# A fused two-layer transformer on one core: the opening of its second attention, reordered

## The reference, cut to what matters

```python
x = x + L0_attn(ln(x))   # 16 heads of 8, rope, softmax, then a relu FFN
x = x + L0_ffn(ln(x))    # router picks 2 of 16 experts: 128 -> 512 -> 128, relu
x = x + L1_attn(ln(x))   # causal attention with an added "incidence" bias
x = x + L1_ffn(ln(x))    # router picks 2 of 8 experts, exact gelu
```

```python
logits = q @ k.T * 8 ** -0.5 + (r @ (J w).T) * decay[h] ** (tq - tk) * bias_scale[h]   # bias only for tq > tk
attn   = softmax(where(tk > tq, -inf, logits))
```

## Time and profile before

| what | us |
|---|---|
| three runs | 1718.39, 1709.72, 1717.89; median 1717.89 |
| the profiled execution | 1723.04 |
| its span, first to last instruction | 1721.3 |
| TensorE busy | 1436.0 (83%), mean granted clock 0.92 |
| VectorE busy | 1237.4 (72%) |
| ScalarE busy | 934.4 (54%) |
| GpSimd busy | 694.0 (40%) |

### The profile page before, as it was taken

The page is one execution under the profiler, slowest core; times in us unless marked ns, Lnnn a source line. Parts: engine busy times, 40 slices in busy tenths (PEclk is TensorE's granted clock), DMA queues, the critical chain, the costliest instruction groups (busy, mean ns, idle before and its releaser), DMA issues. The chain is left out here.

```text
span 1721.3 us, 38302 instructions
## 1 busy us (share of the span) xinstructions
PE 1436.0 (83%) x11726; PEld 955.6 (56%) x11726; DVE 1237.4 (72%) x4218; ACT 934.4 (54%) x1914; POOL 694.0 (40%) x812
## 2 busy tenths in 40 slices
PE   3899999999999945999248989898898987838993
PEld 1224333443333335999126667676776765628993
DVE  5777888888886544555578697888989796635555
ACT  2477777777775712665235555556555553305561
POOL 3123443534422334555225344535454460234552
PEclk8799999999998977999669999999999999968997
DMA  6211111111111061222453444444344453042225
GB/s 159 73 43 61 47 55 47 51 59 51 55 48 41 14 233 51 73 72 64 138 171 122 131 143 138 132 137 143 117 136 140 136 151 115 14 135 62 71 73 165
DMA packets 122424, 166.42 MB, mean 97 GB/s; under 512 B 21490, under 2 KB 96018, under 8 KB 121586
## 3 DMA queue, kind: packets, MB, share of 16 engines
q1 hardware_dynamic: 113330, 145.69, 29.2%
q0 software_dynamic: 8896, 18.30, 3.2%
HBM read 116.04 MB, written 47.60 MB: 95 GB/s over the span
## 5 line engine op out<-in xcount | busy, mean ns | idle before, releaser
L1124 DVE TENSOR_REDUCE a_M<-a_F 128x1 f32<-128x512 f32 x512 | 325.3, 682 | 87.5 <-PE a_F L1318 85.4
L1025 ACT ACTIVATE L_W<-a_ST 128x512 f32<-128x512 f32 x512 | 276.8, 595 | 89.5 <-PE a_ST L1359 88.8
L2042 ACT ACTIVATE L_W<-c_ST 128x1024 f32<-128x1024 f32 x160 | 163.0, 1019 | 175.4 <-PE c_ST L2432 129.2
L2654 ACT ACTIVATE L_hT<-L_P,L_W1s 128x128 f32<-128x128 f32 x600 | 171.4, 367 | 143.1 <-PE L_P L2735 110.9
L2640 POOL DMA_INDIRECT L_yd<-L_ys,L_di x150 | 163.5, 1090 | 151.2 <-DVE L_ys L2686 147.4
L489 POOL DMA_INDIRECT L_xd<-L_XN,L_place_i x128 | 124.6, 973 | 144.4 <-issue 93.5
L1359 PE MATMUL a_ST<-L_W 74*128 74x512 bf16 x512 | 167.0, 390 | 14.2 <-ACT L_W L1025 7.5
L1318 PE MATMUL a_F<-L_W 72*128 72x512 bf16 x512 | 165.0, 398 | 7.9 <-DVE a_M L1124 7.1
L2726 PE MATMUL L_P<-L_xT,L_W1s 128*128 128x128 f32 x1200 | 161.1, 278 | 0.0
L2735 PE MATMUL L_P<-L_W,L_hT 128*128 x1200 | 159.2, 276 | 0.1
L2431 PE MATMUL c_ST<-ident,c_SD 128*128 128x128 f32 x512 | 147.5, 288 | 13.5 <-ACT L_W L2042 13.5
(11 more groups left out here) (430 smaller groups left out, 3090.5 us busy)
## 6 DMA issues: line engine op xcount, KB each, us to landing
c_QS<-c_q SPq DMA_DIRECT2D x32, 504.0 KB
c_QS<-c_rd SPq DMA_DIRECT2D x32, 378.0 KB
L_xg<-L_xd SPq DMA_DIRECT2D x150, 64.5 KB
L_W<-a_q SPq DMA_DIRECT2D x32, 288.0 KB
L_W<-a_k SPq DMA_DIRECT2D x96, 96.0 KB
L_W<-c_k SPq DMA_DIRECT2D x96, 96.0 KB
L_W<-in_L_w SPq DMA_DIRECT2D x8, 1024.0 KB, 12.9
c_QI<-c_r SPq DMA_DIRECT2D x32, 216.0 KB
```

What stands on the lines that cost most here:

```text
L1025: act.activation(PT[:, j, kk, :], ST[:, kk, :], ACT.Exp).then_inc(sem(exped), 1)
L1124: dve.tensor_reduce(M[:, t, h:h + 1], FB[n % BANKS][:, :], AX_X, ALU.max).then_inc(sem(maxed), 1)
L2042: act.activation(PT[:, j, :, :], ST[:, :, :], ACT.Exp).then_inc(sem(exped), 1)
L2654: act.activation(hT[:, n % 2, f, :], PS[2 + 2 * (n % 2) + f // 2][:, (f % 2) * P:(f % 2 + 1) * P], func, bias=W1s[:, n % WB, F + f:F + f + ...
```

## The change

Four things change. (1) The loads of the first two of the five batches are issued ahead of the wait for the weights; the other three stay behind it. (2) VectorE runs mix(0) and mix(1) ahead of the products of batch 0, and not between measure(1) and scale(1). (3) In the opening SyncE stores three of the five pieces of lines, waits for r and w, issues the points of quad 0, then stores the two rd pieces, and fills the c_wd stack and the c_rd stack with a wait for the rd stores between; that is the order in which `run` has it for the later batches. (4) In `run`, the points of quad 1 of the next batch are issued (after the wait for the logits of quad 3) ahead of the wait for quad 2's scores and of quad 2's stacks, and no longer ahead of quad 3's.

```diff
             sp.dma_start(rd_d[:, :, 0:P].rearrange("a p s -> p a s"), QS[0:LINES, 0:PARTS, 0:P]).then_inc(weights, 16)
+
+            def load_results(n):
+                i = B - LATER + n
+                for k in range(CH):
+                    sp.dma_start(mixing[:, n, k, :, :], results[:, k, i * T:(i + 1) * T, :]).then_inc(mix_loaded[n], 16)
+
+            for n in range(2):
+                load_results(n)
             sp.wait_ge(weights, 16 * NW)
...
-            for n in range(LATER):
-                i = B - LATER + n
-                for k in range(CH):
-                    sp.dma_start(mixing[:, n, k, :, :], results[:, k, i * T:(i + 1) * T, :]).then_inc(mix_loaded[n], 16)
+            for n in range(2, LATER):
+                load_results(n)
             store_qk(0)
             stack_qk(0, 0)
-            store_lines(0, range(5))
+            store_lines(0, range(3))
             lines_stored(0, 0)
             stack_points(0, 0)
+            store_lines(0, range(3, 5))
             lines_stored(0, 1)
+            stack_written(0, 0)
             lines_stored(0, 2)
-            stack_lines(0, 0)
+            stack_read(0, 0)
             stack_points(0, 1)
...
                     for g in range(1, NQ):
-                        if g == NQ - 1:
+                        if g == 2:
                             quad_logits(i, 3)
                             stack_points(i + 1, 1)
                         quad_scored(i, g)
...
+            for n in range(2):
+                mix(n)
             for z in range(2):
                 products(dve, 0, z)
                 sums(0, z)
...
             measure(1)
-            for n in range(2):
-                mix(n)
             scale(1)
             for n in range(2, LATER):
                 mix(n)
```

## The result

| | before | after |
|---|---|---|
| median of 21 runs each, us | 1721.30 | 1713.14 |
| lowest and highest | 1708.77, 1738.44 | 1702.66, 1729.96 |
| ratio, 95% interval | | 0.9952, 0.9929 to 0.9975 |
| profiled execution, its span | 1723.04, 1721.3 | 1720.21, 1718.1 |
| second attention, from the first weight's load to the expert layer's first weights | 677.4 | 665.0 |

A forecast was written before the change was run, and what follows sets the result against it. Opening bound by no engine, its end set by the c_rd stack's DMA; later batches keep TensorE and VectorE nearly gapless. Terms +0.1, +0.1, 0, +0.4, -0.8 sum to -0.2 us: 1717.7 us from 1717.89, range 1709.5 to 1723.0.

The forecast's parts named there:

- signs of being wrong: Forecast falls if batches from 934 us on differ by over 1 us each; other signs covered projections, c_rd stack, first logits.
- the bands given: Signs of being right in the opening: c_rd stack issued at 879.4 to 880.2, TensorE's first logits at 885.8 to 886.6.
- What bounds the opening: 833 to 886 us: no engine bounds it; the c_rd stack's DMA releases the first logits, VectorE has 3.39 us of slack.
- Four loads: Loads ahead of the weights' wait may delay the last weights' landing: +0.1 us, bounds 0 and 3.5.
- rival 1: Early loads crowd the weights in the opening and delay the projections: up to 3.5 us, 1721.2 us; chance 0.16.
- Sixteen adds in the gap: Adds in VectorE's gap before batch 0's products: products slip 0.5 us, mostly absorbed; +0.1 us, bounds 0 and 1.3.
- The adds gone from before the scale: VectorE, 874.22 to 880.34 us: it waits for GpSimd's rstd instead; value 0, bounds 0 and 0.3 us.
- rival 3: The adds before the scale were the gate: 6.1 us go, 1711.8 us; chance 0.06.
- First stacks: Opening's stores and stacks in the batches' order: c_rd stack 0.4 us later, bounds 0.6 sooner and 1.0 later.
- Points of quad 1 in each batch: Issued before quad 2's scores in each batch, they save at most the 1.2 us of waits: -0.8 us, bounds -1.2 and 0.
- Rival 4: The new median falls on the level of one earlier run, with nothing gained by the change: 1709.5 us; chance 0.14.

The follow-up runs named there:

- e2: Kernel before with parts 1 to 3 (early loads, early adds, first stacks' order), run's order as before; 1722.57 us, ratio 1.0040.
- e3: Kernel before with only the early loads and early adds (parts 1 and 2); ratio 0.9953, median of all ten runs 1718.05 us.
- e6: Changed kernel with the next batch's quad 2 points also ahead of quad 3's scores; 1708.17 us, ratio 0.9931 against the kernel before.
- e4: Kernel before with only the first stacks in the batches' order (part 3); ratio 1.0022.
- e10: Kernel before, but in run(6) quad 1's points go between the two halves of quad 2's stacks; one run, 1715.45 us beside 1721.06.
- e5: Kernel before with quad 1's points ahead of quad 2's scores in run(6) alone; 1714.33 us, ratio 0.9961.

## Why the prediction was right and wrong, by its steps

That the time lies in the range is luck. The forecast started from a median of three runs that was 3.4 us too low, and its change was -0.2 us where 8.2 were measured; the low end that caught the result was there for spread alone. Its own signs of being wrong point the same way: I had no mechanism by which a batch could differ by more than 1 us, and the last one differed by 7.4; and no wait for c_KI was to stay, where 4.5 us in 4 did. Counted as in the trace before, the c_rd stack went out at 880.4 and the first logits started at 887.4, 0.2 and 0.8 us later than the bands given.

- *What bounds the opening*: right. The c_rd stack released the first logits after as before, and VectorE had slack (4.52 us).
- *Four loads*: right in size. The first projections came 10.16 us after the first weight's load, against 10.05 before; rival 1 (crowded weights) is out: no trace has them later than 10.65.
- *Sixteen adds in the gap*: right in the changed kernel, low in the others. The adds took 4.54 us (4.5 said), ended 0.4 us behind ScalarE's fourth copy, whose end used to start the products, and the line stage took part of the slip back: 0.1 us is left at the w store in the changed kernel (0.1 said), 0.5 to 0.8 in e2, e3 and e6. The TENSOR_SCALAR beside GpSimd's subtractions took 1.10 us, 0.226 elsewhere. In the changed kernel the square began at 862.92, ahead of GpSimd's 863.21, and took its usual 0.56. In e6, where GpSimd's first two subtractions ran from 849.38 to 852.03, the subtraction and the square both began behind that start:

```profile
849.62 1.39 DVE L1629 TENSOR_TENSOR c_line<-c_prod 128x384 f32<-128x384 f32 x1
851.04 1.40 DVE L1631 TENSOR_TENSOR c_prod<-c_line 128x384 f32<-128x384 f32 x1
```

  In e2 and e3 the square alone did, and took 1.39. The Trainium skill's rule on the port pair that VectorE and GpSimd share (SBUF — State Buffer, section "SBUF: two separate sides") would have them block, and these traces agree with it. The TENSOR_SCALARs behind them then block less often, three in the changed kernel, two in e2 and e3 and one in e6, which is how part of the slip comes back.
- *The adds gone from before the scale*: right, 6.25 us of waiting for rstd in their place, and 0.3 us from the shorter select (rival 3 is out).
- *First stacks*: right, 0.3 later in the changed kernel, 0.4 to 0.7 in e4 and e2 (0.4 said).
- *Points of quad 1 in each batch*: wrong in size, and this is the miss of the sum. I wrote that they can bring "at most the 1.2 us of waits", read from a list of TensorE's waits that ended at 1400 us, while the second attention runs on to 1510. Taken from 895 to 1500 us, the same view of the kernel before has

```profile
PE c_INC L2400 <- DMA c_KI<-c_w: 9.3, 5, 6.3
```

and the longest of them is the one that the change removes. In run(6) nothing is left to prepare for a batch i + 2, so TensorE reaches the next batch's quad 1 sooner: 1433.1 us, 12.5 after the first of quad 2's stacks goes out (1420.57); in run(0) it reached it 15.8 us after (963.90 to 979.66). SyncE's fixed order, 6 us of quad 2's stacks and then 3 of points, with 7 to 9 us to land, just fits the long run and misses the short one. The second part of the miss is the clock: I priced waits at their own length, and behind 6.25 us of idleness TensorE ran 4 us at half its clock, which makes 7.4 us of 6.25.

With -6.25 and some 1 to 2 us of clock in place of -0.8 the same sum gives 6.7 to 7.7 us less, and the measured difference is 8.2 (4.3 to 12.2 by its interval). Rival 4, that the median might read 1709.5 us by spread alone, gave the range its low end, and not a mechanism.

## What to carry to other kernels

Take the list of waits over the whole stage, and by loop iteration: the last iterations have less work between the same waits, and it is there that a fixed issue order starves the engine. Price a stall of TensorE above its own length, since the clock may have fallen when it ends. Work moved into an idle gap gains only if what stood behind it was not waiting for something else; here that was GpSimd's rstd, 0.48 us behind the adds.

## What the runs showed of the hardware

Behind a wait of 2.38 us the granted clock was 0.50 over the next 4 us (e10), and the same 33 matmuls were done in those 4 us as behind 6.25 us (before). It does not follow the length of the wait alone. Behind the 4.13 us of e4, and behind 2.75 us at the first logits of quad 2 in e3, the first matmuls still ran at 0.39 us, and the clock fell after them (0.57 and 0.59 over the 4 us from there on); behind waits at the same place of 1.83 us (before), 2.00 (e5) and 2.05 (after) it stayed at 1.00, and behind 1.83 us in e2 it was 0.69.

A VectorE instruction of 0.56 us on two SBUF tensors took 1.39 to 1.40 when it began while GpSimd was subtracting SBUF tensors (e2, e3, e6). Single executions of one kernel, before, ranged from 1708.77 to 1738.44 us in 21 runs, so that the first three (1709.72 to 1718.39) had put its median 3.4 us too low. Most of such spread goes with the granted clock: 12 to 16 us for each 0.01 of its mean over a run.
